# Storing the bf16 terms of q and k once and loading them twice, with the early stores of an attention and expert kernel in another order

## The chip, the cores and the metric

The kernel runs on one core of a Trainium2 chip. The core has a tensor engine (PE, with PEld for its weight loads), a vector engine (DVE), a scalar engine (ACT), GpSimd (POOL), a sync engine (SP) that does little but issue DMAs, and 16 DMA engines that all queues share. The metric is the device time of one execution in microseconds.

## What is computed

One transformer block with adaptive layer norm, on 1024 tokens of width 256. Cut to what matters:

```python
h = layernorm(x) * (1 + ca) + sa
q = (h @ Wq.T + bq) * 16 ** -0.5          # 16 heads of 16
k = h @ Wk.T + bk
v = h @ Wv.T + bv
scores = q @ k.T + slopes * -abs(i - j)   # 1024 x 1024 for each head
x = x + ga * (softmax(scores) @ v @ Wo.T + bo)
h = layernorm(x) * (1 + cb) + sb
x = x + gb * top4_of_16_experts(h)
```

## The kernel before

The first 44 us project x into q, k and v. The attention runs from there to about 255 us, head by head; the experts take the rest, and no line of theirs is touched.

**Terms.** q and k are split into three bf16 terms each (`qk_part[:, w, f, part, :]`, w 0 for q and 1 for k, f the half of the heads, 16 partitions a head). Products of terms stand in for a float32 product. The terms go from SBUF to DRAM (`q_rows`, `k_rows`: 96 rows of 1024 bf16 for each head, six blocks of 16) and come back with all rows of one head on neighbouring partitions. Which term stands in which block is told by `Q_PARTS` and `K_PARTS`: term 0 of q is stored three times, term 1 twice, term 2 once. `load_max(g)` (L502, L503) brings the first 64 rows twice, to partitions 0 to 63 and 64 to 127 of `qx` and `kx`, for the pass that finds the row maxima. `load_st(h)` (L509, L511) brings all 96 rows to `q_st` and to two copies in `k_st`, for the transposed scores. `load_al(h)` (L517) adds 24 rows of a bias from `al_rows`, which one store (L531) writes for all heads. `place_rows(g)` (L549) copies the row maxima, split by POOL in `split_rows` (L866), from `m_row` into two rows of `q_st`.

**Who stores what.** Heads 0 and 1: SP (`store_head`, L490, for the first four blocks, `store_terms` for the last two). Heads 2 to 7: ACT between its copies of v (four blocks), SP later (the last two). Heads 8 to 15: POOL, four DMAs in each of steps 0 to 2. Lines 455 to 456 are `store_term`.

**Order.** Every engine has its own program, run in order, with semaphore waits. The loop `steps` goes through c = -2 to 15. In step c PE computes the transposed scores of head c (L1460), the product with v (L1479), and the maxima scores of head c+2 (L1443, from the second pair of p on) and of head c+1 (the last two tiles, at p = 0). After the first two tiles of head c+2 it transposes the maxima of head c+1 (L1490); ACT copies them (L687), POOL splits them, SP places them. PE waits for `mx_in` (the four DMAs of `load_max`) before the first L1443 of a head and for `st_in`, `al_ld` and `m_in` before the first L1460. In step c SP issues, in this order: `load_st(c+1)`, `load_al(c+1)`, the store of head c-1's output (`os_rows`, L542), `place_rows(c+1)`, `load_max(c+3)`. DMAs of one engine go to one queue and are worked off in order on each DMA engine. From step 7 on POOL also loads the weights of one expert in each step (L901, L903; three in step 13), 672 KB each.

Of the kernel before, what the change touches and what calls it, by code (L numbers as in the profile page):

```python
# [10 lines left out]
BF16 = mybir.dt.bfloat16  # L11
# [6 lines left out]
P = 128  # L18
T = 1024
# [3 lines left out]
H = 16  # L23
# [14 lines left out]

Q_PARTS = (0, 1, 0, 1, 2, 0)
K_PARTS = (0, 0, 1, 1, 0, 2)  # L40
R_MX = 4 * D
# [71 lines left out]
def adaln_block(nc, a, out):  # L113
    with ExitStack() as ctx:
# [9 lines left out]

        q_rows = dram("q_rows", [H, 6 * D, T], BF16)
        k_rows = dram("k_rows", [H, 6 * D, T], BF16)
        al_rows = dram("al_rows", [6, H * NT, T], BF16)
# [324 lines left out]

        def store_term(eng, w, f, first, last, g):

            rows, part = ((q_rows, Q_PARTS[g]), (k_rows, K_PARTS[g]))[w]
            return eng.dma_start(rows[first:last, D * g:D * g + D, :],
                                 qk_part[D * first - P * f:D * last - P * f, w, f, part, :])

        @block.sync
        def _(sp):  # L460
# [23 lines left out]
            def store_head(h, w):  # L484

                rows, p0 = (q_rows, k_rows)[w], D * h
                for k in range(2):
                    src = (qk_part[p0:p0 + D, 0, 0, 0:2, :] if w == 0 else
                           qk_part[p0:p0 + D, 1, 0, k:k + 1, :].broadcast_to([D, 2, T]))
                    sp.dma_start(rows[h, 2 * D * k:2 * D * k + 2 * D, :].rearrange("(g r) t -> r g t", g=2),  # L490
                                 src).then_inc(qk_head[h], 16)

            def store_terms(n, first, last, terms):

                for w in range(2):
                    for g in terms:
                        store_term(sp, w, 0, first, last, g).then_inc(qk_stored[n], 16)
# [26 lines left out]
            for h in range(2):  # L524
                sp.wait_ge(qk_head[h], 16 * 4)
                load_max(h)
            sp.wait_ge(qk_split, 4)
            store_terms(0, 0, 2, (4, 5))
            sp.wait_ge(al_done, 1)
            sp.wait_ge(sign_done, 1)  # L530
            sp.dma_start(al_rows.rearrange("g r n -> r g n"), al_part[:]).then_inc(al_stored, 16)  # L531
            sp.wait_ge(qk_stored[0], 16 * 4)
            load_st(0)
            sp.wait_ge(al_stored, 16)
            load_al(0)
            load_st(1)
            load_al(1)

            def store_o(h):

                sp.wait_ge(o_evac, h + 1)
                sp.dma_start(os_rows[h].rearrange("r (g n) -> g r n", g=G), o_sb[:, h % 2, :]).then_inc(o_stored[h % 2], 16)  # L542

            def place_rows(g):

                sp.wait_ge(m_done, g + 1)
                for r in range(R_M):
                    to = R_QK + R_AL + r
                    sp.dma_start(q_st[to:to + 1, g % SLOTS, :].rearrange("p (i x) -> p i x", i=NT),  # L549
                                 m_row[:, r, :]).then_inc(m_in, 16)  # L550

            def step(c):
                if c == H - 2:
                    store_o(c - 1)
# [10 lines left out]
                if 0 <= c + 1 < H:  # L565
                    place_rows(c + 1)
                if 2 <= c + 3 < H:
                    if c == -1:
                        sp.wait_ge(qk_terms, 16 * 8)
                    if c + 3 == HT:  # L570
                        sp.wait_ge(qk_stored[2], 16 * 12)
                    sp.wait_ge(max_used, NT * c + 2 * NT)
                    load_max(c + 3)
                if c == -1:
                    sp.wait_ge(qk_split, 4)
                    store_terms(1, 2, HT, (4, 5))

# [24 lines left out]
        def _(act):  # L602
# [66 lines left out]
            for g in range(4):  # L669
                act.wait_ge(pe_group, V0 + g + 1)  # L670
                act.copy(v_all[:, 2 * g:2 * g + 2, :].rearrange("p t e -> p (t e)"), ps[:, bank_of[V0 + g], :]).then_inc(act_evac, 1)
                act.wait_ge(qk_second, 4)
                for w in range(2):
                    store_term(act, w, 0, 2, HT, g).then_inc(qk_terms, 16)
            make_bias_t(1)
# [103 lines left out]
        def _(pool):  # L779
# [75 lines left out]
            stage_v(1)  # L855
            for n in range(4, 8):
                rest_of(n, (n - 4) // 2, 1, n % 2)
                if n > 4:
                    third_part(n - 1, (n - 5) // 2, 1, (n - 1) % 2)

            def split_rows(g):
# [6 lines left out]

            split_rows(0)
            third_part(7, 1, 1, 1)  # L870
# [50 lines left out]
            def step(c):  # L921
# [8 lines left out]
                if 0 <= c < 3:  # L930
                    pool.wait_ge(qk_split, 8)
                    for w in range(2):
                        for g in (2 * c, 2 * c + 1):
                            store_term(pool, w, 1, HT, H, g).then_inc(qk_stored[2], 16)
                if c == 3:
# [7 lines left out]
                if c == C_EXP:  # L943

                    for h in range(2):
                        pool.wait_ge(qk_head[h], 16 * 4)
                    for n in range(3):
                        pool.wait_ge(qk_stored[n], 16 * (4, 4, 12)[n])
                    pool.wait_ge(qk_terms, 16 * 8)
                    pool.wait_ge(al_stored, 16)  # L950
                    pool.wait_ge(wo_done, 1)
                    pool.wait_ge(pe_group, N_GROUPS)
# [345 lines left out]
        def _(pe):  # L1298
# [147 lines left out]
            def scores_t(c, j, ch):  # L1446
# [3 lines left out]
                if u == 0:  # L1450
                    pe.wait_ge(st_in[s], 48 * (c // SLOTS) + 48)
# [205 lines left out]
```

## Time and profile before

| | us |
|---|---|
| median of 3 runs | 493.79 (493.55 to 493.92) |
| profiled execution, its own time | 489.35 |
| its span in the trace | 487.5 |
| PE busy | 401.6 (82% of the span) |
| DVE / ACT / POOL busy | 284.8 / 237.0 / 289.4 |
| DMA moved | 64.50 MB, mean 132 GB/s |

The profiled execution is 4.4 us shorter than the median; 1.85 us of its time lie outside the span. Differences worked out in the trace are therefore added to the median. PE is the busiest engine, but its share is a mean over the whole span. In the start, and at the first scores of a head, PE stands idle until a transfer lands; how often is read from PE's timeline, and what the transfer had to wait for from SP's timeline and the DMA share.

### The profile page before, as it was taken

The numbers are of one execution on the slowest core, as the hardware profiler recorded it, in microseconds if no ns is written. First come the engines' busy times: TensorE is split into PE (matmuls) and PEld (weight loads), VectorE is DVE, ScalarE is ACT, GpSimd is POOL, SyncE is SP. The second block draws the span as 40 slices with busy tenths as digits, with TensorE's granted clock in tenths as the row PEclk, the third lists the DMA queues.
The fourth block names the chain that finished last, engine by engine and source line by source line (L and its number), as shares of the span: only waits on it lengthen the run. The fifth ranks groups of instructions, "written<-read, shape, count | busy, mean of one in ns | idle before, by whom it ended". The sixth has DMA issues, their size and how long they took to land.

```text
span 487.5 us, 10785 instructions
## 1 busy us (share of the span) xinstructions
PE 401.6 (82%) x3712; PEld 218.0 (45%) x3714; DVE 284.8 (58%) x646; ACT 237.0 (49%) x503; POOL 289.4 (59%) x291
## 2 busy tenths in 40 slices
PE   4898749999999999999876627799899997999700
PEld 1764214344444444444435514366565554656400
DVE  3951948888998998999313784233333333333256
ACT  1273826777777777777870330233333333333211
POOL 5657617778889877777266001466566566665422
PEclk9598959999999999999995855899999999999955
DMA  7624735776333566658569900222222222232074
GB/s 217 257 39 153 239 117 137 176 190 203 109 106 105 155 170 168 170 159 239 165 151 298 279 5 2 73 77 73 64 84 66 75 67 66 75 76 56 0 273 157
DMA packets 38184, 64.50 MB, mean 132 GB/s; under 512 B 8177, under 2 KB 20903, under 8 KB 38014
## 3 DMA queue, kind: packets, MB, share of 16 engines
q1 hardware_dynamic: 25198, 34.95, 22.7%
q0 software_dynamic: 11584, 26.89, 21.6%
q10 hardware_dynamic: 1360, 2.10, 1.3%
q8 instruction: 27, 0.44, 0.4%
q14 instruction: 15, 0.12, 0.1%
HBM read 47.78 MB, written 18.01 MB: 135 GB/s over the span
## 4 chain that ended last, share of the span: by engine, by line
PE 50%; DVE 15%; DMA 13%; issue 8%; SPq 6%; ACT 5%; another core or an unknown queue 1%; POOL 0%; DVEq 0%; POOLq 0%; ACTq 0%
PE ps L1618 13%; PE ps L1460 7%; PE ps L1628 7%; PE ps L1479 7%; PE ps L1443 4%; ACT probs L703 3%; DVE x_sb L1290 3%; PE ps L1609 3%; DMA al_rows<-w_gu 3%; DVE junk L1096 3%; DMA x_sb<-in_x 2%; PE ps L1602 2%; DMA hT<-inv_rows 2%; PE ps L1465 2%; SPq L517 2%
## 5 line engine op out<-in xcount | busy, mean ns | idle before, releaser
L1096 DVE CUSTOM_DVE_ANT_0 junk<-ps,bias_t 128x1024 bf16<-128x1024 f32 x128 | 155.3, 1219 | 32.6 <-PE ps L1443 31.4
L703 ACT ACTIVATE probs<-ps 128x512 f32<-128x512 f32 x256 | 137.1, 603 | 47.5 <-DVE ps L1107 39.6
L1460 PE MATMUL ps<-q_st,k_st 122*32 122x512 bf16 x1024 | 84.5, 390 | 7.1 <-DMA q_st<-m_row 4.5
L1618 PE MATMUL ps<-w_gu,probs 128*128 x188 | 81.8, 558 | 0.0
L972 POOL DMA_INDIRECT probs<-xn_rows,bias_t x47 | 48.0, 1020 | 53.4 <-DVE bias_t L1259 38.6
L979 POOL DMA_INDIRECT z_rows<-probs,bias_t x47 | 48.1, 1023 | 49.9 <-DVE probs L1282 33.2
L1479 PE MATMUL ps<-probs,v_st 128*32 128x256 f32 x1024 | 66.7, 380 | 0.7 <-ACT probs L703 0.7
L797 POOL TENSOR_SCALAR bias_t<-dist,slopes 128x1920 f32<-128x1920 f32 x13 | 66.5, 5112 | 0.0
L1275 DVE TENSOR_TENSOR probs<-probs,ps 128x224 f32<-128x224 f32 x47 | 18.2, 387 | 81.5 <-ACT probs L765 56.6
L1443 PE MATMUL ps<-kx,qx 64*128 64x512 bf16 x256 | 44.2, 393 | 9.2 <-DMA kx<-k_rows 4.7
L754 ACT ACTIVATE probs<-ps,modc 128x128 f32<-128x128 f32 x47 | 21.5, 457 | 61.1 <-PE ps L1602 40.0
L1628 PE MATMUL ps<-w_dn,probs 112*128 x188 | 48.5, 380 | 0.5 <-ACT probs L760 0.5
L1460 PEld LDWEIGHTS ps<-q_st,k_st 122*32 122x32 bf16 x1024 | 23.6, 95 | 51.1 <-ACT probs L703 24.6
L1628 PEld LDWEIGHTS ps<-w_dn,probs 112*128 112x128 f32 x188 | 35.4, 189 | 20.5 <-issue 17.8
L765 ACT ACTIVATE probs<-ps 128x224 f32<-128x224 f32 x47 | 16.8, 358 | 53.8 <-PE ps L1618 46.3
L1618 PEld LDWEIGHTS ps<-w_gu,probs 128*128 128x128 f32 x188 | 32.1, 190 | 19.4 <-issue 18.4
L1479 PEld LDWEIGHTS ps<-probs,v_st 128*32 128x32 f32 x1024 | 30.6, 110 | 18.2 <-ACT probs L703 1.0
L1282 DVE TENSOR_TENSOR probs<-ps,gates 128x256 f32<-128x256 f32 x47 | 19.9, 424 | 16.2 <-remote 9.1
L1107 DVE TENSOR_TENSOR ps<-ps,bias_d 128x128 f32<-128x128 f32 x64 | 18.8, 294 | 16.6 <-PE ps L1460 16.6
L1443 PEld LDWEIGHTS ps<-kx,qx 64*128 64x128 bf16 x256 | 11.8, 93 | 36.7 <-issue 18.5
L1609 PE MATMUL ps<-ident,probs 128*112 128x128 f32 x94 | 19.1, 285 | 9.6 <-DVE probs L1275 6.0
L1465 PE MATMUL ps<-bias_d,ident 128*32 128x128 f32 x512 | 25.7, 277 | 0.0
(202 smaller groups left out, 486.1 us busy)
## 6 DMA issues: line engine op xcount, KB each, us to landing
k_st<-k_rows SPq DMA_DIRECT2D x32, 192.0 KB, 5.0
qx<-q_rows SPq DMA_DIRECT2D x32, 128.0 KB, 2.6
w_gu<-in_gate_proj POOLq DMA_DIRECT2D x16, 224.0 KB, 4.2
w_gu<-in_up_proj POOLq DMA_DIRECT2D x16, 224.0 KB, 5.1
w_dn<-in_down_proj POOLq DMA_DIRECT2D x16, 224.0 KB, 6.4
q_st<-q_rows SPq DMA_DIRECT2D x16, 192.0 KB, 3.7
kx<-k_rows SPq DMA_DIRECT2D x32, 64.0 KB, 2.7
os_rows<-o_sb SPq DMA_DIRECT2D x14, 128.0 KB
```

The lines of the kernel that those rows point to most:

```text
L703: act.activation(probs[:, j % 4, CH * ch:CH * ch + CH], ps_st[(NU * c + u) % 3], ACT.Exp).then_inc(exp_done, 1)
L797: pool.tensor_scalar(bias_t[:, h % 2, :], dist[:], slopes[:, h:h + 1], None, ALU.mult).then_inc(bias_p_done, 1)
L972: pool.indirect_dma_start(xg[:, n % 4, :], None, xn_rows, bass.IndirectOffsetOnAxis(ap=tab_i[:, n, 0:1].bitcast(U32), axis=0), bounds_chec ...
L979: pool.indirect_dma_start(z_rows, bass.IndirectOffsetOnAxis(ap=tab_i[:, n, 1:2].bitcast(U32), axis=0), y_sb[:, n % 4, :], None, bounds_che ...
L1096: dve.tensor_tensor_reduce(junk[:, n % 2, :], ps_max[n % 2].rearrange("p b n -> p (b n)"), bias_t[:, g % 2, off:off + T], 1.0, -3.0e38, AL ...
L1443: last = pe.matmul(ps_max[n % 2][:, r, :], qx[k, s, q * P:q * P + P], kx[k, s, :], start=True, stop=True)
L1460: last = pe.matmul(ps_st[n % 3][32 * g:32 * g + 32, :], k_st[0:R_ALL, ch, s, r:r + 32], q_st[0:R_ALL, s, CH * ch:CH * ch + CH], start=True ...
L1465: last = pe.matmul(ps_st[n % 3][32 * g:32 * g + 32, t * P:t * P + P], ident[:, 32 * g:32 * g + 32], bias_d[:, c % D_SLOTS, :], start=False ...
L1479: last = pe.matmul(ps_o[32 * g:32 * g + 32], v_st[:, c % 2, j, :], probs[:, j % 4, QG * g:QG * g + QG], start=(j == 0), stop=(j == NT - 1))
L1609: last = pe.transpose(ps[0:IH, 4 + (c - 1) % 2, kk * P:kk * P + P], hid[:, (c - 1) % 2, kk * IH:kk * IH + IH], ident[:])
L1618: last = pe.matmul(ps[:, 2 + c % 2, 0:2 * INTER], xT[:, c % 2, kk, :], w_gu[:, bass.ds(e, 1), kk, :].rearrange("p x n -> p (x n)"), start= ...
L1628: last = pe.matmul(ps[:, 6 + c % 2, 0:E], hidT[0:IH, c % 2, kk, :], w_dn[0:IH, bass.ds(e2, 1), kk, :].rearrange("p x n -> p (x n)"), start ...
```

## The change

- `q_rows` keeps four blocks a head, `k_rows` three: every term once, but term 0 of q twice. Terms 0 and 1 of q stand interleaved (row 2d + g), so that one DMA with runs of 4 KB stores both.
- The loads make the copies. For q: `q_rows[g, 0:2 * D, :]`, 32 rows, with a leading dimension of size 2 and stride 0 in front, onto 64 partitions. For k: 32 rows, each followed by a dimension of size 2 and stride 0. `load_max` stays at four DMAs of the same bytes; `load_st` becomes five DMAs from three.
- Heads 0 and 1: one store each for q and k instead of two. Heads 2 to 7: ACT issues three stores instead of eight, SP three instead of four. Heads 8 to 15: POOL issues two in each of steps 0 to 2 instead of four.
- `al_rows` is stored in two parts: 16 partitions (heads 0 and 1) right after `load_max(0)`, the other 112 after `load_al(1)`, just ahead of `load_max(2)`.
- `place_rows(0)` moves ahead of `load_st(1)`; POOL's `split_rows(0)` moves two tiles of splitting up.

```diff
-            return eng.dma_start(rows[first:last, D * g:D * g + D, :],
-                                 qk_part[D * first - P * f:D * last - P * f, w, f, part, :])
+        def store_q_pair(eng, f, first, last):
+            return eng.dma_start(q_rows[first:last, 0:2 * D, :].rearrange("h (d g) t -> h d (g t)", g=2),
+                                 qk_part[D * first - P * f:D * last - P * f, 0, f, 0:2, :].rearrange("p g t -> p (g t)"))
...
             def load_max(g):
                 for r in range(2):
-                    sp.dma_start(qx[R_MX * r:R_MX * r + R_MX, g % 2, :], q_rows[g, 0:R_MX, :]).then_inc(mx_in[g % 2], 16)
+                    sp.dma_start(qx[R_MX * r:R_MX * r + R_MX, g % 2, :],
+                                 q_rows[g, 0:2 * D, :].unsqueeze(0).broadcast_to([2, 2 * D, T])).then_inc(mx_in[g % 2], 16)
                     sp.dma_start(kx[R_MX * r:R_MX * r + R_MX, g % 2, :],
-                                 k_rows[g, 0:R_MX, CH * r:CH * r + CH]).then_inc(mx_in[g % 2], 16)
+                                 k_rows[g, D:3 * D, CH * r:CH * r + CH].unsqueeze(1)
+                                 .broadcast_to([2 * D, 2, CH])).then_inc(mx_in[g % 2], 16)
             def load_st(h):
-                sp.dma_start(q_st[0:R_QK, s, :], q_rows[h]).then_inc(st_in[s], 16)
+                sp.dma_start(q_st[0:R_MX, s, :],
+                             q_rows[h, 0:2 * D, :].unsqueeze(0).broadcast_to([2, 2 * D, T])).then_inc(st_in[s], 16)
+                sp.dma_start(q_st[R_MX:R_QK, s, :], q_rows[h, 2 * D:4 * D, :]).then_inc(st_in[s], 16)
                 for ch in range(NCH):
-                    sp.dma_start(k_st[0:R_QK, ch, s, :], k_rows[h]).then_inc(st_in[s], 16)
+                    sp.dma_start(k_st[0:R_MX, ch, s, :],
+                                 k_rows[h, D:3 * D, :].unsqueeze(1).broadcast_to([2 * D, 2, T])).then_inc(st_in[s], 16)
+                sp.dma_start(k_st[R_MX:R_QK, :, s, :],
+                             k_rows[h, 0:2 * D, :].unsqueeze(1).broadcast_to([2 * D, NCH, T])).then_inc(st_in[s], 16)
...
+            sp.wait_ge(qk_head[0], 16 * 2)
+            load_max(0)
+            sp.wait_ge(al_done, 1)
+            sp.wait_ge(sign_done, 1)
+            store_al(0, 0, 2)
+            sp.wait_ge(qk_head[1], 16 * 2)
+            load_max(1)
+            sp.wait_ge(qk_split, 4)
+            store_third(0, 0, 2)
+            sp.wait_ge(qk_stored[0], 16 * 3)
+            load_st(0)
+            sp.wait_ge(al_stored[0], 16)
+            load_al(0)
+            place_rows(0)
+            load_st(1)
+            load_al(1)
+            store_al(1, 2, H)
```

SP at the start, before, from the loads of head 1's maxima on (the numbers are the shape of the destination):

```order
L502 DMA qx<-q_rows 64x1024 [waits qk_head1]
L503 DMA kx<-k_rows 64x512
L502 DMA qx<-q_rows 64x1024
L503 DMA kx<-k_rows 64x512
L456 DMA q_rows<-w_gu 2x16x1024 [waits qk_split]
L456 DMA q_rows<-w_gu 2x16x1024
L456 DMA k_rows<-w_gu 2x16x1024 x2
L531 DMA al_rows<-w_gu 128x6x1024 [waits sign_done,al_done]
L509 DMA q_st<-q_rows 96x1024 [waits qk_stored0]
L511 DMA k_st<-k_rows 96x1024 x2
L517 DMA k_st<-al_rows 24x1x1024 [waits al_stored]
```

SP at the same place, after (`w_gu` holds `qk_part` and `al_part` at this time):

```order
L542 DMA al_rows<-w_gu 16x6x1024 [waits sign_done,al_done]
L510 DMA qx<-q_rows 64x1x1024 [waits qk_head1]
L512 DMA kx<-k_rows 64x1x512
L510 DMA qx<-q_rows 64x1x1024
L512 DMA kx<-k_rows 64x1x512
L461 DMA q_rows<-w_gu 2x16x1024 [waits qk_split]
L461 DMA q_rows<-w_gu 2x16x1024
L456 DMA k_rows<-w_gu 2x16x1024
L519 DMA q_st<-q_rows 64x1x1024 [waits qk_stored0]
L521 DMA q_st<-q_rows 32x1024
L523 DMA k_st<-k_rows 64x1x1024 x2
L525 DMA k_st<-k_rows 32x2x1024
```

The part of `al_rows` for heads 0 and 1 now stands ahead of head 1's loads, and one store of a term is gone. Next on SP, before, what stands between the bias rows of head 0 and the loads of head 2's maxima:

```order
L517 DMA k_st<-al_rows 24x1x1024
L509 DMA q_st<-q_rows 96x1024
L511 DMA k_st<-k_rows 96x1024 x2
L517 DMA k_st<-al_rows 24x1x1024 x2
L549 DMA q_st<-m_row 1x8x128 [waits m_done]
L549 DMA q_st<-m_row 1x8x128
L502 DMA qx<-q_rows 64x1024 [waits max_used,qk_terms]
```

And after:

```order
L532 DMA k_st<-al_rows 24x1x1024
L549 DMA q_st<-m_row 1x8x128 [waits m_done]
L549 DMA q_st<-m_row 1x8x128
L519 DMA q_st<-q_rows 64x1x1024
L521 DMA q_st<-q_rows 32x1024
L523 DMA k_st<-k_rows 64x1x1024 x2
L525 DMA k_st<-k_rows 32x2x1024
L532 DMA k_st<-al_rows 24x1x1024 x2
L542 DMA al_rows<-w_gu 112x6x1024
L510 DMA qx<-q_rows 64x1x1024 [waits max_used,qk_terms]
```

The placing of head 0's maxima moved ahead of head 1's loads, and the large part of `al_rows` came in front of head 2's first load.

## Rows read from the trace of the kernel before

**Rows 1.** The page, its slices of 12.2 us: PE busy and granted clock.
```profile
PE   4898749999999999999876627799899997999700
PEclk9598959999999999999995855899999999999955
```

**Rows 2.** PE's timeline, start and length in us; before the first L1490 (44 to 72).
```profile
44.56 0.91 PE L1443 MATMUL ps<-kx,qx 64*128 64x512 bf16 x4 [2.39 <-DMA kx<-k_rows]
...
63.77 0.61 PE L1443 MATMUL ps<-kx,qx 64*128 64x512 bf16 x2 [0.44 <-DVE mx L1096]
68.61 1.47 PE L1460 MATMUL ps<-q_st,k_st 122*32 122x512 bf16 x12 [4.24 <-DMA q_st<-m_row]
...
71.86 1.03 PE L1443 MATMUL ps<-kx,qx 64*128 64x512 bf16 x4 [0.91 <-DMA kx<-k_rows]
```

**Rows 3.** PE's timeline: the first maxima scores of heads 3, 4, 5, 8, 9 and 15.
```profile
84.66 0.61 PE L1443 MATMUL ps<-kx,qx 64*128 64x512 bf16 x4
...
97.06 0.61 PE L1443 MATMUL ps<-kx,qx 64*128 64x512 bf16 x4 [0.95 <-DMA kx<-k_rows]
...
108.94 0.60 PE L1443 MATMUL ps<-kx,qx 64*128 64x512 bf16 x4 [0.47 <-DMA kx<-k_rows]
...
143.19 0.60 PE L1443 MATMUL ps<-kx,qx 64*128 64x512 bf16 x4
...
154.59 0.61 PE L1443 MATMUL ps<-kx,qx 64*128 64x512 bf16 x4
...
222.93 0.60 PE L1443 MATMUL ps<-kx,qx 64*128 64x512 bf16 x4
```

**Rows 4.** The chain of waits, in order of time.
```profile
34.18 0.30 SPq L490
34.53 2.17 DMA k_rows<-w_gu
...
48.28 13.19 DMA al_rows<-w_gu
```

**Rows 5.** SP's own waits, 30 to 135 us: total, times, longest.
```profile
SPq L509 <- DMA k_rows<-w_gu: 8.5, 1, 8.5
```

**Rows 6.** SP's timeline of DMA issues, step 6: start, length.
```profile
140.44 0.32 SPq L509 DMA_DIRECT2D q_st<-q_rows  x1
...
141.75 1.58 SPq L517 DMA_DIRECT2D k_st<-al_rows  x2
143.59 0.58 SPq L542 DMA_DIRECT2D os_rows<-o_sb  x1
145.52 1.36 SPq L549 DMA_DIRECT2D q_st<-m_row  x2
146.92 0.51 SPq L502 DMA_DIRECT2D qx<-q_rows  x1
```

**Rows 7.** Windows: span, busy time of five engines, PE clock, share of 16 DMA engines, GB/s.
```profile
15.00:16.00 1.00, 1.00 (x8) 1.00 (x6) 1.00 (x4) 0.00 (x0) 0.00 (x0) 0.50 1.04 419
...
56.00:58.00 2.00, 1.20 (x6) 0.27 (x5) 1.81 (x5) 1.65 (x4) 2.00 (x2) 1.00 0.31 119
141.90:142.90 1.00, 1.00 (x26) 0.34 (x16) 1.00 (x4) 0.69 (x2) 0.00 (x0) 1.00 0.93 338
144.00:145.20 1.20, 1.14 (x25) 0.62 (x28) 1.20 (x4) 0.64 (x3) 0.41 (x2) 1.00 0.23 64
145.30:146.60 1.30, 1.30 (x24) 0.50 (x16) 1.01 (x2) 1.30 (x3) 1.30 (x2) 1.00 0.26 84
```

**Rows 8.** The page's DMA issues: size of one, median us from issue to landing.
```profile
qx<-q_rows SPq DMA_DIRECT2D x32, 128.0 KB, 2.6
w_gu<-in_gate_proj POOLq DMA_DIRECT2D x16, 224.0 KB, 4.2
```

**Rows 9.** POOL's timeline: the split of the first maxima, and the first expert load.
```profile
60.86 0.42 POOL L867 TENSOR_TENSOR m_row<-m_f,m_row 8x128 bf16<-8x128 f32 x1
...
162.56 0.81 POOL L901 DMA_DIRECT2D w_gu<-in_gate_proj  x1
```

More of the change, by code:

```diff
@@ L35 @@
 HT = P // D
[L39 to L40 removed]
+K_ROW = (D, 2 * D, 0)
+Q_ROW = {0: 2 * D, 2: 3 * D}
 R_MX = 4 * D
@@ L317, in adaln_block @@
         al_done = sem("al_done")
-        al_stored = sem("al_stored")
+        al_stored = [sem(f"al_stored{n}") for n in range(2)]
         v_done = sem("v_done")
@@ L451, in tiles, with store_k, store_q @@
                 tile(MAX_TILES // 4, k - MAX_TILES // 4 * 4)
-        def store_term(eng, w, f, first, last, g):
-            rows, part = ((q_rows, Q_PARTS[g]), (k_rows, K_PARTS[g]))[w]
-            return eng.dma_start(rows[first:last, D * g:D * g + D, :],
-                                 qk_part[D * first - P * f:D * last - P * f, w, f, part, :])
+        def store_k(eng, f, first, last, part):
+            b = K_ROW[part]
+            return eng.dma_start(k_rows[first:last, b:b + D, :], qk_part[D * first - P * f:D * last - P * f, 1, f, part, :])
+        def store_q(eng, f, first, last, part):
+            b = Q_ROW[part]
+            return eng.dma_start(q_rows[first:last, b:b + D, :], qk_part[D * first - P * f:D * last - P * f, 0, f, part, :])
+        def store_q_pair(eng, f, first, last):
+            return eng.dma_start(q_rows[first:last, 0:2 * D, :].rearrange("h (d g) t -> h d (g t)", g=2),
+                                 qk_part[D * first - P * f:D * last - P * f, 0, f, 0:2, :].rearrange("p g t -> p (g t)"))
         @block.sync
@@ L484, in store_head @@
             def store_head(h, w):
[L486 to L497, printed above, removed]
+                if w == 0:
+                    store_q_pair(sp, 0, h, h + 1).then_inc(qk_head[h], 16)
+                else:
+                    sp.dma_start(k_rows[h, D:3 * D, :].rearrange("(g r) t -> r g t", g=2),
+                                 qk_part[D * h:D * h + D, 1, 0, 0:2, :]).then_inc(qk_head[h], 16)
@@ L499, in load_max, with store_third @@
+            def store_third(n, first, last):
+                for part in (0, 2):
+                    store_q(sp, 0, first, last, part).then_inc(qk_stored[n], 16)
+                store_k(sp, 0, first, last, 2).then_inc(qk_stored[n], 16)
             def load_max(g):
                 for r in range(2):
-                    sp.dma_start(qx[R_MX * r:R_MX * r + R_MX, g % 2, :], q_rows[g, 0:R_MX, :]).then_inc(mx_in[g % 2], 16)
+                    sp.dma_start(qx[R_MX * r:R_MX * r + R_MX, g % 2, :],
+                                 q_rows[g, 0:2 * D, :].unsqueeze(0).broadcast_to([2, 2 * D, T])).then_inc(mx_in[g % 2], 16)
@@ L523, in _, with store_al @@
                     store_head(h, w)
[L524 to L542, printed above, removed]
+            def store_al(n, first, last):
+                r = slice(NT * first, NT * last)
+                sp.dma_start(al_rows[:, r, :].rearrange("g r n -> r g n"), al_part[r]).then_inc(al_stored[n], 16)
             def place_rows(g):
@@ L672, in _ @@
                 act.wait_ge(qk_second, 4)
-                for w in range(2):
-                    store_term(act, w, 0, 2, HT, g).then_inc(qk_terms, 16)
+                if g == 0:
+                    store_q_pair(act, 0, 2, HT).then_inc(qk_terms, 16)
+                elif g < 3:
+                    store_k(act, 0, 2, HT, g - 1).then_inc(qk_terms, 16)
             make_bias_t(1)
@@ L855, in _ @@
             stage_v(1)
[L856 to L859, printed above, removed]
             def split_rows(g):
@@ L867, in split_rows @@
                 pool.tensor_tensor(m_row[:, 1, :], m_f[:], m_row[:, 0, :], ALU.subtract).then_inc(m_done, 1)
-            split_rows(0)
+            for n in range(4, 8):
+                rest_of(n, (n - 4) // 2, 1, n % 2)
+                if n > 4:
+                    third_part(n - 1, (n - 5) // 2, 1, (n - 1) % 2)
+                if n == 6:
+                    split_rows(0)
             third_part(7, 1, 1, 1)
```

39 lines of the change are left out of this document (23 added, 16 removed).

## The prediction

> **What bounds the kernel now.** I read the page's slices first: PE is at nine tenths nearly everywhere, with a weak stretch at 49 to 73 us, where the clock is also at its lower level [rows 1]. PE's timeline then says what it waits for. Between 44 and 72 us it waits four times for DMAs or maxima; the largest is 4.24 us until head 0's maxima are placed, then 0.91 us for head 2's loads [rows 2]. After that the first maxima scores of a head (I call this moment X, with X0 = 71.86 for head 2) mark the pace: 84.66, 97.06, 108.94, and from there 11.4 us a head (154.59 - 143.19), up to X13 = 222.93 [rows 2, 3]. Waits of 0.95 and 0.47 us for DMAs stand at the second and third; the later ones have none [rows 3]. So DMAs decide the start, and PE with its partners the rest, as long as each head's loads land within its 11.4 us.
>
> The margin for that is read from SP's timeline. In the step with X = 143.19, `load_st` begins at X - 2.8, `place_rows` at X + 2.3, `load_max` at X + 3.7 [rows 3, 6]. Its four issues of some 0.6 us and a landing of 2.6 us [rows 8] end about X + 8.5, so 3 us are to spare.
>
> **How many DMA engines one transfer uses.** The windows show it [rows 7]. While `load_st` runs (96 rows outermost) the share of the 16 engines is 0.93. While `os_rows` is stored (destination 4x32x256) it is 0.26, which is four engines. While the bias rows run (source 6x4x1024) it is 0.23, near six engines with gaps. So a transfer is split along its outermost dimension, and a 4 there gives four engines. The new q loads read 2x32x1024: the copy dimension is outermost. I conclude two engines for each 128 KB. The new k loads have 32 rows outermost and keep 16.
>
> What the trace can't show is which two. The Trainium skill ("DMA: Bandwidth & Descriptors", section on why a DMA increments its semaphore by 16) has the count as the largest number up to 16 that divides the outermost size of both sides, and the engines as the lowest-numbered ones. The trace agrees on the count, with 0.26 for four.
>
> That small transfers share the same engines follows from a wait as well. SP waits 8.5 us for its term stores, until 57.1 us [rows 5]. By then two-engine stores of 4 x 64 KB (128 KB on each of the two), six-engine stores of 8 x 192 KB by ACT (256 KB) and 48 KB of loads were queued from about 38 us on. If all fall on the same engines, 432 KB (442 kB) in 19 us are 23.3 GB/s: one engine's pace. The other paces are 24.0 (119 GB/s at a share of 0.31), 21.1 (338 at 0.93, taken as 16 engines) and 26.2 (419 over 16) [rows 7]. The first is that of a few leftover engines late in the store of `al_rows`, which landed after 13.19 us although most of the rest was idle [rows 4, 7]. I take 25.0, the middle of 24.0 and 26.2, since no limit that all 16 share should bind two.
>
> **The change, part by part.** All of it is counted as KB on each of the two lowest engines.
>
> *Removed.* Stores: ACT 128 KB instead of 256, SP's third terms of heads 0 and 1 96 instead of 128, POOL 1792 KB instead of 3072 in three steps. Issues: ACT five fewer, POOL six fewer. Neither engine is waited for before the copy and split of head 0's maxima, which ends at 61.28 [rows 9] and follows PE's scores, so this is worth nothing.
>
> *Loads of one head, steady.* Before: `load_max` 2 x (8 + 4) = 24 KB, `load_st` 36, bias rows 16, `os_rows` 32, so 108 KB or 4.4 us of 11.4. After: `load_max` 2 x (64 + 4) = 136, `load_st` 64 + 4 + 8 + 8 + 8 = 92, bias rows 16, `os_rows` 32: 276 KB = 282.6 kB, at 25.0 GB/s 11.3 us. All of it is waited for within one head, in one queue, so the head can't be shorter than this and some 0.2 us of hand-over: 11.5 us. `load_st`'s two further issues (0.3 to 0.8 us each, by L509 and the bias rows [rows 6]) fall into 1.35 us in which SP waits for the maxima, at no cost; bounds 0 to 0.3 us, since `load_max` has its 3 us to spare.
>
> *X0.* The first loads are issued at 36.3 (34.18 for the single k store and its 2.1 us landing, [rows 4]), their data begin 1.5 us later. `load_max(0)` needs 139.3 kB = 5.6 us of engine time beside ACT's 131 kB = 5.2 us: landing between 43.5 (served first) and 49 (served last). Before, 24 KB beside the same queue landed 3 us later than alone (44.56, [rows 2]), so I take 47.5. Then `load_max(1)` 136, bias rows 12 and third terms 96 KB, 250 kB = 10.0 us, stored at 58 (before 57.1). `load_st(0)` and `load_al(0)` take 2.3 + 1.5 us of issue, until 62; the maxima, 3 us late with PE but two tiles of POOL's work earlier, are there at 61.5 (before 61.3, [rows 9]). Placing takes 1.4 us and lands near 66, while PE ends its own maxima scores near 67.5 (64.38 + 3). So the wait of 4.24 us goes, given back by the late start. Next on SP: `load_st(1)`, `load_al(1)`, the rest of `al_rows`, until 67.5, then `load_max(2)`. On the engines: 4.4 us for head 0 (to 64), 4.4 for head 1 (65 to 69), 84 KB of `al_rows` 3.4 (to 72.6), `load_max(2)` 5.6: 78.2, landed 79.0. X0 moves from 71.86 to 79.0: **+7.1 us**. At 26.2 GB/s +6.3, at 24.0 +7.5.
>
> *X0 to X3.* POOL's stores add 112 KB on each engine over three steps, 1.5 us a step: 13.0 us each, against 12.80, 12.40 and 11.88: **+1.9**. The six-engine third terms of heads 2 to 7 (48 KB, 2.0 us) fall into the first, where PE is just as late.
>
> *X3 to X7.* 4 x 11.5 against 45.65: **+0.4**.
>
> *X7 to X13.* POOL loads one expert a step, 672 KB over 16 engines = 43 kB = 1.7 us, first issued at 162.56 [rows 9]. Queues take turns on an engine, so a head needs 13.2 us against 11.39. The first load comes late in its step, so I count 5.5 of 6: **+10**. Cover for none of this is left, as PE, DVE and SP all wait for the same loads.
>
> Sum: 7.1 + 1.9 + 0.4 + 10 = 19.4. The profiled run would come from 489.35 to 508.8, the median from 493.79 to **513.2 us**. At 24.0 GB/s a head needs 12.0, 13.6 and 13.8 us, in sum +27 (521); at 23.3 +32 (526); at 26.2 11.0, 12.5 and 12.7, in sum +14 (508). These rates are the largest unknown. Nothing behind 255 us changes.
>
> **The rivals.**
>
> *A, the copies cost nothing (faster).* The stride-0 dimension isn't what the transfer is split by, and the loads use 16 engines as before. For it: same bytes, same row sizes. Against it: the 0.26 for an outermost 4 [rows 7]. Then maxima of head 0 are placed at about 60, `load_max(2)` is issued at 64.5 to 67, behind 1.34 MB of `al_rows` at 338 GB/s (4 us): landing 71, X0 -0.9; of the 2.9 us by which the next three heads exceed 11.4 each, a third returns. 493.8 - 2 = 491.8. The point from which it decides: `load_max` landing in under 3 us.
>
> *B, two engines, but quick ones.* Over 26 GB/s each, the loads of a head fit into 11.4 us with the expert's too; only the start is lost, +5 to +7, with up to 7 us from the experts' steps: 499 to 508. For it: 419 GB/s over 16 [rows 7] was shared. Against it: 24.0 in the same group. The Trainium skill (the same page, "Specifications") has about 27 GiB/s, 29 GB/s, for one engine. By it 282.6 kB take 9.7 us and an expert's 1.5, so nothing is lost after X3, and the time would be 499 as its estimate. No row here reaches it.
>
> *C, slower engines.* At 21.1 GB/s a head needs 13.6 us, 15.6 with the expert: 4 x 2.2 + 5.5 x 4.2 + 9 + 9.7 = +50, 544. Also into this case falls a clock that drops in PE's waits, as in the slices that follow the idle stretches of the start [rows 1, 2].
>
> **How the numbers follow.** The forecast (508 to 528) gets 0.62, B (498 to 508) 0.20, C (over 528) 0.08, A 0.10. A range of 500 to 528 leaves out A, C and a small part of B, 0.2 in all. A measurement of this kernel tells about 0.2% from no change. Slower: all but A and a remnant, 0.90. Faster 0.08, same 0.02.
>
> **What would show it.** In the new trace: landing of `qx<-q_rows` at 5 us and more instead of 2.6; a DMA share near 0.13 while it alone runs; PE waiting for `kx` or `qx` ahead of each head's first maxima scores, small for heads 6 to 9, near 2 us for heads 10 to 15; first scores of head 0 at 47 to 48, X0 near 79; no wait for `m_row` at the first L1460. X13 - X7 well over 68.3. If qx lands in under 3 us, A holds and the whole sum falls; if the heads run at 11.4 us to the end, B.

## The result, and the profile after

| | before | after |
|---|---|---|
| median | 493.67 us (4 runs) | 537.33 us (535.9 to 541.92, 4 runs) |
| profiled execution, its span | 489.35, 487.5 | 537.87, 536.1 |
| mean granted clock | 0.903 | 0.872 |
| first maxima scores of head 2 (X0) | 71.86 | 82.75 |
| X0 to X3, X3 to X7, X7 to X13 | 37.1, 45.7, 68.3 | 41.2, 49.5, 90.9 |
| last product with v (before L1479, after L1508) | 253.49 | 305.44 |

The ratio is 1.0897 (95%: 1.0841 to 1.0954): slower, as forecast, but by 43.7 us where 19.4 were forecast, and outside the range of 500 to 528. Some executions fall into a slower state of the chip, so the ratios here and below are of the fast ones alone, and only e6's trace is of a slow one (533.03 us). In the numbering of the changed kernel the maxima scores are L1472 (before L1443), the transposed scores L1489 (L1460), the loads of `qx` and `kx` L510 and L512.

The page's slices, PE busy and granted clock, to set beside [rows 1]: the weak stretch at the start is longer, and from the middle of the attention on (slices 15 to 22, 188 to 295 us) few nines are left.

```profile
PE   4994728979899877869594864679999989898900
PEclk8696957989999997979798995589999979999955
```

PE's waits between 30 and 310 us (total, times, longest). The first stands in the place of 4.7 us in four waits for `kx` in before. The second is at the last head, where before had none; the 4.24 us for `m_row` at the first L1460 [rows 2] are gone:

```profile
PE ps L1472 <- DMA kx<-k_rows: 44.7, 13, 10.8
PE ps L1489 <- DMA q_st<-m_row: 7.2, 1, 7.2
```

PE's timeline (start, length, wait in brackets): the first scores of head 0 (44.56 in [rows 2]), the first L1489, which no longer waits for `m_row`, then X0, X4, X7, X9, X13, and the last head's L1489.

```profile
49.30 1.04 PE L1472 MATMUL ps<-kx,qx 64*128 64x512 bf16 x4 [7.85 <-DMA kx<-k_rows]
69.63 1.47 PE L1489 MATMUL ps<-q_st,k_st 122*32 122x512 bf16 x12
82.75 1.04 PE L1472 MATMUL ps<-kx,qx 64*128 64x512 bf16 x4 [10.77 <-DMA kx<-k_rows]
136.89 0.60 PE L1472 MATMUL ps<-kx,qx 64*128 64x512 bf16 x4 [1.48 <-DMA kx<-k_rows]
173.48 0.60 PE L1472 MATMUL ps<-kx,qx 64*128 64x512 bf16 x4 [0.53 <-DMA kx<-k_rows]
203.74 1.04 PE L1472 MATMUL ps<-kx,qx 64*128 64x512 bf16 x4 [5.72 <-DMA kx<-k_rows]
264.37 1.04 PE L1472 MATMUL ps<-kx,qx 64*128 64x512 bf16 x4 [5.46 <-DMA kx<-k_rows]
292.85 1.47 PE L1489 MATMUL ps<-q_st,k_st 122*32 122x512 bf16 x12 [7.20 <-DMA q_st<-m_row]
```

A window (columns as in [rows 7]) in which a q load runs alone:

```profile
170.00:171.00 1.00, 1.00 (x16) 0.37 (x16) 0.90 (x3) 0.80 (x2) 1.00 (x1) 1.00 0.13 51
```

The share of 0.13 is two of 16 engines, and 51 GB/s over two are 25.5 GB/s each. The number of engines and their rate were therefore right (25.0 had been taken); what was built on them fell short.

Where the 48.6 us between the spans lie: X0 +10.9, X0 to X3 +4.1, X3 to X7 +3.9, X7 to X13 +22.6, from X13 to the last product with v +10.5 (41.07 against 30.56), behind that -3.3 (230.7 against 234.0). The -3.3 are two parts. From the last product with v to the first expert's matmul it takes 46.4 us where before takes 53.9: PE's 4.45 us wait for `attT` is gone, as PE comes later itself. From there to the end it takes 4.1 us more, for a reason that was not looked for. So most of what the last head loses by its wait of 7.2 us comes back.

### The profile page after: what moved, and what is told of

The parts are those of the page before. It is cut to its first block, busy times and chain, and to the rows that moved or that the text cites. A ratio compares the mean times of both kernels' runs of the same rounds, so it can differ in the third digit from the quotient of the medians.

```text
span 536.1 us, 10802 instructions
## 1 busy us (share of the span) xinstructions
PE 410.1 (76%) x3712; PEld 220.1 (41%) x3714; DVE 284.8 (53%) x646; ACT 239.3 (45%) x503; POOL 285.9 (53%) x285
## 3 DMA queue, kind: packets, MB, share of 16 engines
q10 hardware_dynamic: 850, 1.31, 0.8%
## 4 chain that ended last, share of the span: by engine, by line
PE 37%; DMA 24%; DVE 13%; SPq 11%; issue 5%; ACT 4%; POOL 3%; another core or an unknown queue 3%; ACTq 0%; POOLq 0%; DVEq 0%
DMA kx<-k_rows 16%; PE ps L1647 12%; PE ps L1657 6%; PE ps L1508 3%; PE ps L1638 3%; PE ps L1489 3%; SPq L510 3%; DVE x_sb L1319 3%; DVE junk L1125 3%; PE ps L1472 2%; DMA k_rows<-w_gu 2%; SPq L512 2%; SPq L549 2%; PE ps L1631 2%
## 5 line engine op out<-in xcount | busy, mean ns | idle before, releaser
L1489 PE MATMUL ps<-q_st,k_st 122*32 122x512 bf16 x1024 | 86.0, 405 | 9.5 <-DMA q_st<-m_row 7.2
L1647 PE MATMUL ps<-w_gu,probs 128*128 x188 | 83.2, 566 | 0.0
L1472 PE MATMUL ps<-kx,qx 64*128 64x512 bf16 x256 | 45.3, 406 | 49.5 <-DMA kx<-k_rows 44.7
L1508 PE MATMUL ps<-probs,v_st 128*32 128x256 f32 x1024 | 71.1, 400 | 0.7 <-ACT probs L729 0.7
L780 ACT ACTIVATE probs<-ps,modc 128x128 f32<-128x128 f32 x47 | 21.5, 457 | 58.7 <-PE ps L1631 47.8
L1489 PEld LDWEIGHTS ps<-q_st,k_st 122*32 122x32 bf16 x1024 | 23.4, 98 | 52.5 <-issue 22.7
L1472 PEld LDWEIGHTS ps<-kx,qx 64*128 64x128 bf16 x256 | 11.0, 94 | 78.3 <-DMA kx<-k_rows 40.6
L1508 PEld LDWEIGHTS ps<-probs,v_st 128*32 128x32 f32 x1024 | 32.1, 115 | 20.3 <-issue 2.8
L887 POOL CAST m_row<-m_f 8x128 bf16<-8x128 f32 x16 | 4.5, 280 | 53.4 <-ACT m_f L713 53.4
L1494 PE MATMUL ps<-bias_d,ident 128*32 128x128 f32 x512 | 27.0, 288 | 0.0
```

The lines of the kernel that those rows point to most:

```text
L780: act.activation(xT[:, (c + 1) % 2, 0, :], ps[:, 0, 0:P], ACT.Identity, bias=modc[:, 2, 0:1], scale=modc[:, 3, 0:1]).then_inc(xT_act, 1)
L1472: last = pe.matmul(ps_max[n % 2][:, r, :], qx[k, s, q * P:q * P + P], kx[k, s, :], start=True, stop=True)
L1489: last = pe.matmul(ps_st[n % 3][32 * g:32 * g + 32, :], k_st[0:R_ALL, ch, s, r:r + 32], q_st[0:R_ALL, s, CH * ch:CH * ch + CH], start=True ...
L1494: last = pe.matmul(ps_st[n % 3][32 * g:32 * g + 32, t * P:t * P + P], ident[:, 32 * g:32 * g + 32], bias_d[:, c % D_SLOTS, :], start=False ...
L1508: last = pe.matmul(ps_o[32 * g:32 * g + 32], v_st[:, c % 2, j, :], probs[:, j % 4, QG * g:QG * g + QG], start=(j == 0), stop=(j == NT - 1))
L1647: last = pe.matmul(ps[:, 2 + c % 2, 0:2 * INTER], xT[:, c % 2, kk, :], w_gu[:, bass.ds(e, 1), kk, :].rearrange("p x n -> p (x n)"), start= ...
```

## The experiments

The kernels ran on several chips, on which the kernel before takes 477 to 497 us in the median; each is compared with runs of before on its own chip. The numbers used across chips are differences in the attention, X's above all: the pace of 11.39 us a head is the same on all of them. "Ready" is when PE was free for the first maxima scores (42.17 in before: 44.56 less its wait of 2.39). The ratio of e11 is that of 508.8 to 492.8 us and has no interval. The stages vary from trace to trace: X3 to X7 is 45.7 and 47.1 us in two traces of before, and 49.5 and 51.1 in after and e4, whose programs are the same up to there.

| | ratio to before (95%) | X0 - ready | X0 to X3 | X3 to X7 | X7 to X13 |
|---|---|---|---|---|---|
| before | | 29.7 | 37.1 | 45.7 | 68.3 |
| after | 1.0897 (1.0841 to 1.0954) | 41.3 | 41.2 | 49.5 | 90.9 |
| e1_q_two_loads | 1.0131 (1.0070 to 1.0192) | 34.1 | 40.8 | 45.6 | 68.3 |
| e2_before_max2 | 1.0788 (1.0709 to 1.0866) | 43.7 | 45.0 | 51.4 | 81.1 |
| e3_before_both2 | 1.0982 (1.0894 to 1.1069) | 44.0 | 44.5 | 53.2 | 88.2 |
| e4_after_experts_late | 1.0535 (1.0458 to 1.0613) | 41.5 | 41.9 | 51.1 | 73.3 |
| e5_before_max2_early_load | 1.0732 (1.0647 to 1.0817) | 43.2 | 47.8 | 57.1 | 76.6 |
| e6_after_early_load | 1.0987 (1.0886 to 1.1088) | 41.9 | 45.1 | 56.9 | 90.4 |
| e7_two_loads_al_behind | 1.0070 (1.0017 to 1.0123) | 31.2 | 40.9 | 45.6 | 68.3 |
| e8_two_loads_max_first | 1.0122 (1.0084 to 1.0161) | 27.0 | 44.4 | 45.6 | 70.2 |
| e11_before_max2_three | 1.03 | 43.0 | 41.6 | 45.5 | 70.3 |
| e12_after_three | 1.0603 (1.0426 to 1.0781) | 41.4 | 38.2 | 48.3 | 84.4 |
| e13_before_join | 1.0000 (0.9928 to 1.0072) | 29.4 | 36.6 | 45.5 | 68.3 |
| e15_two_loads_order_join | 1.0118 (1.0018 to 1.0217) | 27.0 | 45.2 | 45.6 | 70.5 |
| e16_before_order_alone | 1.0140 (1.0076 to 1.0204) | 32.6 | 41.3 | 46.8 | 68.3 |
| e17_two_loads_old_order | 1.0051 (1.0010 to 1.0092) | 28.3 | 40.5 | 45.6 | 68.3 |

### Are the two engines the cause?

```diff
-                    sp.dma_start(qx[R_MX * r:R_MX * r + R_MX, g % 2, :],
-                                 q_rows[g, 0:2 * D, :].unsqueeze(0).broadcast_to([2, 2 * D, T])).then_inc(mx_in[g % 2], 16)
+                    for i in range(2):
+                        b = R_MX * r + 2 * D * i
+                        sp.dma_start(qx[b:b + 2 * D, g % 2, :], q_rows[g, 0:2 * D, :]).then_inc(mx_in[g % 2], 16)
```

and the same in `load_st`, with the wait counts.

> The changed kernel, but each q load with the copy dimension is replaced by two DMAs of 32 rows each, 64 KB, which read the same rows; bytes, stores and order stay as changed, and SP issues two DMAs more in load_max and one more in load_st. Theory (the two engines that the copy dimension leaves to a transfer are the cause): with 32 rows outermost each part spreads over 16 engines, load_max lands in 2 to 3 us again, heads run at 11.4 us (X7 to X13 68 to 70 us against 90.9), the first maxima scores of head 2 stand at 71 to 73, and the time is 489 to 495. Rival (the added issues of load_st on SP, the early store of a part of al_rows, or the k loads with their copy dimension inside are the cause): these all stay or grow, and the time stays over 515.

It is the cause of most of it: every head from X3 on takes 11.4 us again. Issue to landing of the q loads, by this kernel's page (the page of after gives no median for them):

```profile
qx<-q_rows SPq DMA_DIRECT2D x64, 64.0 KB, 2.1
```

But X0 still came at 80.4, not 71 to 73, with a wait of 7.2 us (4.1 of the 8.5 us against before are a later ready, 46.27), and the kernel stays 1.3% slower. This rest is taken up below. The reverse edits, the copy dimension put into the loads of the kernel before:

> The kernel before with one edit: the two q loads of load_max read 32 rows with a leading copy dimension of 2 instead of 64 rows; the blocks of the kernel before hold these same terms in the same order, so the result is the same, and so are bytes and number of DMAs. Theory (load on the two engines, as a sum for each head): load_max 136 KB, load_st 36, bias rows 16, output 32, 220 KB or 225 kB on each of the two, at the 25.5 GB/s that two engines showed 8.8 us, which fits into a head of 11.4. So X3 to X7 stays at 45 to 47 us, X7 to X13 is 69 to 76, head 2's first maxima scores come 4 to 8 us later, and the time is 498 to 508. Rival (not the sum but each transfer of its own is what holds PE up, as load_max lands late whenever it takes 5 us and more): waits for qx and kx at every head, X3 to X7 over 49, time over 515.

> The kernel before with both q loads, of load_max and of load_st, read with the leading copy dimension; load_st gains one DMA for its last 32 rows. Stores, k loads and the order of stores stay as before. Theory (the two engines): 220 KB and 62 more in load_st, 280 KB a head on each of the two, as in the changed kernel: heads of 12 us and more, X3 to X7 48 to 51, X7 to X13 87 to 93, time 528 to 540. Rival (the new order of stores or the k loads carry a good part of the loss): under 515.

The second (e3) held in the main: +9.8%, X7 to X13 88.2, X3 to X7 53.2 where 48 to 51 were expected. The loads alone make a loss of the size of the whole. For the first (e2) the rival came true: waits at nearly every head, 51.4 us from X3 to X7, +7.9%. With 220 KB a head on the two engines, 8.8 us of work, a head takes 12.3 to 12.6 us between X4 and X7. The sum, on which the prediction rested, does not explain that. SP's issues in one step of this kernel, and windows of the same step:

```profile
171.91 1.37 SPq L550 DMA_DIRECT2D q_st<-m_row  x2
173.32 0.56 SPq L502 DMA_DIRECT2D qx<-q_rows  x1
175.04 0.48 SPq L504 DMA_DIRECT2D kx<-k_rows  x1
```

```profile
173.00:174.00 1.00, 1.00 (x12) 0.32 (x12) 0.68 (x3) 1.00 (x4) 1.00 (x1) 1.00 0.02 4
174.00:175.00 1.00, 1.00 (x24) 0.56 (x24) 1.00 (x4) 0.68 (x3) 1.00 (x1) 1.00 0.01 4
178.00:179.00 1.00, 1.00 (x20) 0.31 (x8) 0.89 (x3) 1.00 (x3) 1.00 (x1) 1.00 0.13 49
```

```profile
169.93 0.61 PE L1444 MATMUL ps<-kx,qx 64*128 64x512 bf16 x4 [1.14 <-DMA kx<-k_rows]
182.53 0.60 PE L1444 MATMUL ps<-kx,qx 64*128 64x512 bf16 x4 [1.18 <-DMA kx<-k_rows]
```

For 2 us the DMA engines are all but idle; the k loads take the next two, and then only two engines work. They wait for an order of events: at X = 169.93 the previous head's maxima scores are done, POOL splits the maxima, SP places them at X + 2.0 and issues `load_max` at X + 3.4. Its data come from about X + 5 on and need 5.5 us on two engines by themselves (139 kB at 25.5 GB/s); from X + 9 on `load_st` shares the engines. The last has landed at X + 12.6, which is the next X. The buffer is free only after the head before, so each head's load starts from the head's own beginning. This reads as a closed chain of 12.3 to 12.6 us a head. Whether it is the chain or the two engines' load that counts, the next runs test.

### Chain or sum?

First try: `load_max(c+3)` issued ahead of `place_rows(c+1)`.

> The kernel before with the two-engine q loads in load_max alone, as in e2_before_max2, and in each step from 0 on the order of load_max(c+3) and place_rows(c+1) on SP exchanged, so that the load is issued about 3 us earlier after the first maxima scores of a head (X). The result is the same. New theory (a chain, not the sum: X, then split and place of the maxima, then load_max issued at X + 3.4, its data from X + 5.6 on, 6.3 us on two engines, landing at X + 12.4, which is the next X): without the 3 us of placing in it the chain is 9.5 us, shorter than the 11.4 that PE needs, so X3 to X7 falls from 51.4 to 45.6 to 47, X7 to X13 from 81.1 to 69 to 75, and the time from 517.7 to 500 to 508. Rival (the two engines themselves can't deliver a head's loads faster than every 12.3 us, whatever the order): X3 to X7 stays at 49 to 51 and the time over 513.

> The changed kernel with the same exchange: in each step from 0 on SP issues load_max(c+3) before place_rows(c+1). Chain alone as the cause: as in e5_before_max2_early_load, all heads near 11.4 to 11.8 us up to X7, X7 to X13 75 to 80, time 515 to 522. Sum on two engines (276 KB a head, 11.1 us at 25.5 GB/s and 3 us more beside an expert load) as the cause: X3 to X7 stays at 47.5 to 50, X7 to X13 at 84 to 91, and the placed maxima, now behind the load on the same two engines, are waited for instead: time 530 to 540. I expect the sum to hold here, since 11.1 us leave nothing over.

For the changed kernel the second case held, but for X3 to X7, which took 56.9 us where 47.5 to 50 were expected. For e5 the gain did not come, and the rival had only the time right (over 513): X3 to X7 is longer than without the exchange (57.1 against 51.4; one head of 19.2 us in it, the others 12.4 to 12.9), and the pace stays at 12.6 to 12.9 up to X13. PE's wait had only changed its place:

```profile
178.30 0.83 PE L1463 MATMUL ps<-q_st,k_st 122*32 122x512 bf16 x12 [1.13 <-DMA q_st<-m_row]
```

The placed maxima now stand behind the load on the same two engines, and the next head's scores need them. Either order has both transfers in the chain. The experiment didn't take the chain apart; a third buffer does, which lets the load start a head earlier:

```diff
-        qx = sb("qx", [P, 2, T], BF16)
-        kx = sb("kx", [P, 2, CH], BF16)
+        qx = sb("qx", [P, 3, T], BF16)
+        kx = sb("kx", [P, 3, CH], BF16)
...
+                if 3 <= c + 3 < H:
+                    sp.wait_ge(max_used, NT * c + NT)
+                    load_max(c + 3)
```

(at the head of the step, in place of the one at its end that waits for `NT * c + 2 * NT`).

> As e2_before_max2 (the kernel before, load_max with two-engine q loads), but with three buffers for qx and kx instead of two, so that load_max(c+3) no longer waits for the maxima of head c+1 and is issued a whole head before it is needed; bytes, sizes and engines of all transfers stay. e5_before_max2_early_load had left the chain closed, since placed maxima and loads share the two engines and both stood in it. Theory (a chain of release, place, issue and a transfer of 6 us sets 12.3 us a head, not the sum of 220 KB on the two engines, 8.8 us): the waits for kx go from X3 on, X3 to X7 is 45.6 to 46.5 instead of 51.4, X7 to X13 68.3 to 71 instead of 81.1, time 497 to 504. Rival (the two engines are short of capacity at 220 KB a head): X3 to X7 stays at 49 to 51, time over 510.

> The changed kernel with three buffers for qx and kx in the same way; 276 KB a head stay on the two engines. Sum theory: 11.1 us at 25.5 GB/s fit just below the 11.4 that PE needs, so X3 to X7 falls to 46 to 48 from 49.5; beside an expert load (3.1 us more) the sum is 14 us, so X7 to X13 is still 80 to 88 instead of 90.9; time 525 to 534. Chain alone as the cause of the changed kernel's loss after X3: X3 to X7 45.6 to 46 and X7 to X13 68 to 73, time 508 to 516.

With the same 220 KB on the same two engines all waits for `kx` are gone from X1 on and the pace is 11.4 us from X3 to X10: chain, not sum. (The last three heads before X13 take 12.0 to 12.1 us, with waits of 0.7 to 0.8 us for `m_row`. The expected times had a chip in mind on which before takes 480 us; the difference here, 16.0 us, compares with 17 to 24.) In the changed kernel 276 KB are another matter: X3 to X7 goes from 49.5 only to 48.3, no more than traces differ, and X7 to X13 from 90.9 to 84.4. The paces are near those that the sum gave (46 to 48 and 80 to 88), and the waits stand at `m_row` now (0.2 to 3.7 us). The time fell between: 523.05 us, just below the sum's 525 to 534. So in the changed kernel from X3 to X7 no run separates the chain from the load on the two engines; by rate that load is 11.1 us a head, and 12.1 were measured with the third buffer.

### The expert loads

> The changed kernel with all expert loads issued after the loop of steps instead of one in each step from 7 on; what they load is the same, but the first experts wait for it at the end, so the total time says little and the pace of the heads is what counts. Theory (expert loads take their share of the two engines, some 3.1 us a head): X7 to X13 is 6 x 12.0 to 12.4 = 72 to 75 us instead of 90.9, and the wait of 7.2 us for the last head's placed maxima goes. Rival (the later heads are slow for a reason of their own, the clock or the longer queue of output stores): X7 to X13 stays at 85 or more.

X7 to X13 fell by 17.6 us, to 73.3: 2.9 us a head, where the prediction had 1.7. Windows of the changed kernel suggest why, a head's loads and an expert's together (198 to 199), and PE waiting for what was queued behind (202 to 203):

```profile
198.00:199.00 1.00, 0.01 (x4) 0.00 (x0) 0.06 (x2) 1.00 (x4) 0.65 (x2) 1.00 1.04 218
202.00:203.00 1.00, 0.00 (x0) 0.00 (x0) 0.00 (x0) 0.00 (x0) 0.00 (x0) 0.50 0.21 78
```

All 16 engines are busy and move 218 GB/s, 13.6 GB/s each, where alone they reach 25.5. At 13.6 GB/s the 43 kB of an expert's weights on one engine would take 3.2 us, an estimate near the 2.9. That this makes the 2.9 us is a reading of the windows; no run takes it apart. PE's granted clock also falls to 0.50, its 1.2 GHz level, in the longer of these waits, and the first scores after it take 1.04 us for 0.61. The wait of 7 us for the last head's `m_row` did not go (6.95 us here), which had been expected, so the expert loads don't cause it. In the changed kernel SP issues `place_rows(15)` at 284.43, behind POOL's two loads of `attT` (896 KB, 283.55 and 284.13); in before it stood ahead of them (238.32 against 240.17).

### The rest: 1.3% with repaired loads

> As e1_q_two_loads (the changed kernel with each q load as two DMAs of 32 rows), but the large store of al_rows is issued after load_max(2) instead of ahead of it. Theory (what is left of the loss in e1_q_two_loads is head 2's load queued behind 1.34 MB of that store): the wait of 7.2 us before head 2's first maxima scores falls to 3 us or less, and the time by 3 to 5 us against e1_q_two_loads, to about that of the kernel before (+0.1 to 0.7%). Rival (the rest comes from the added issues and the stores of the terms on two engines): less than 1.5 us of change.

> As e1_q_two_loads, but head 2's load_max stands right behind place_rows(0), ahead of load_st(1), load_al(1) and the large store of al_rows. If head 2's load is what PE waits for in the start: it is issued at 67 instead of 72 and finds empty engines, lands at 70 to 71, PE's wait of 7.2 us goes, and the time is 7 to 10 us below e1_q_two_loads, that is 0.2 to 0.9% below the kernel before. Rival (a later wait takes its place, for load_st(1), which is now behind, or for the maxima): 0 to 3 us below e1_q_two_loads.

Moving the large store of `al_rows` behind head 2's load took 2.9 us off X0 - ready and nearly half of the ratio's excess away (1.3% to 0.7%, with intervals that overlap). Moving head 2's load to the front instead gave X0 without a wait (27.0) and gave nearly all of that back one head later, in a wait of 7.8 us for head 1's placed maxima behind that store. Then both halves of the change apart, with a trace of the kernel before from the same chip:

> The kernel before with the change's order alone: al_rows stored in two parts (heads 0 and 1 behind load_max(0), the rest ahead of load_max(2)), place_rows(0) ahead of load_st(1), POOL's split_rows(0) two tiles up; terms stored and loaded as before. The two kernels with repaired q loads and the change's stores reached head 5's first maxima scores 72.1 and 74.9 us after PE was free for the first ones, against 66.8 before. If the order is the cause of that: here 71 to 75 us as well, and 0.7 to 1.5% slower than before. If the stores or the k loads are: 65 to 68 us, and within 0.4% of before.

> The counterpart: terms stored once and q loads as two DMAs of 32 rows (e1_q_two_loads), but the order of before (al_rows in one store behind the terms, place_rows(0) behind load_al(1), split_rows(0) at its old place). If the order was the cause of the rest: head 5's first maxima scores 66 to 68 us after PE was free, time within 0.5% of before. If the stores and more loads are: 71 to 75 us and 0.7 to 1.5% slower.

> The kernel before, unchanged, for a trace from the same chip as the two runs beside it. All kernels that ran on the chips where before takes 480 us needed about 138 us from the first expert's matmul to the last, those on the others 152 to 157. If that is the chip: here either value, with the two beside it at the same; the head's pace, 11.39 us, is the same on all.

The order alone costs 1.4% (0.8 to 2.0), 6.7 us; the terms stored once and loaded with 16 engines, in the order of before, 0.5%, with lower bound 0.1%. So the two halves have their own prices. Both together had 1.3% (e1, 0.7 to 1.9 on another chip), so the prices need not add up. Head 5's first maxima scores stand 73.9 us after ready with the new order alone, 68.8 with the terms alone, 65.6 in before on this chip. A part of the order's price, 3.2 of the 8.4 us, is there at X0, and is seen in windows of 68 to 70 us, e16 first, the kernel before (e18) second:

```profile
68.00:70.00 2.00, 0.00 (x0) 0.00 (x0) 0.00 (x0) 0.00 (x0) 0.00 (x0) 0.50 1.00 314
```

```profile
68.00:70.00 2.00, 1.89 (x24) 0.87 (x24) 1.15 (x2) 0.82 (x2) 0.00 (x0) 0.50 0.60 165
```

Between SP's issue of the store (66.29) and of head 2's load (66.85) nothing waits, and the load's data come behind 1.34 MB; PE waits 7.54 us:

```profile
74.30 1.03 PE L1453 MATMUL ps<-kx,qx 64*128 64x512 bf16 x4 [7.54 <-DMA kx<-k_rows]
```

What the new order wins, maxima of head 0 placed 3.4 us earlier (61.89 against 65.30), is less than that. The other 5.2 us come between X0 and X3, nearly all of them as one wait of 5.01 us for head 5's own `kx` (115.62), when the large store has long landed and POOL's last stores of terms (issued from 106.2 on) are under way. Why it falls there was not looked into. The last two tried to turn the findings into a gain:

> The kernel before, with POOL's two loads of attT (896 KB) issued behind the store of inv_rows instead of ahead of the reciprocals. In the trace of before the chain at the end of the attention runs os_rows, sum_c, inv_rows (5.0 us to landing, behind those 896 KB), hT (8.6 us), attT, and PE waits 4.45 us for it. If the queue in front of inv_rows is what costs: it lands in 2 to 3 us, hT 2 us earlier, PE's wait falls to 1.5 to 3 us, time 0.3 to 0.6% below before. Rival (attT now lands as late as hT did, the bytes before the last one are the same): within 0.2%.

> The changed kernel with each q load as two DMAs (e1_q_two_loads) and three changes of order: load_max(2) right behind place_rows(0) as in e8_two_loads_max_first; the large store of al_rows behind place_rows(1), since it and load_st(1) ahead of it had cost 7.8 us for the placed maxima of head 1; POOL's loads of attT behind the store of inv_rows as in e13_before_join, since place_rows(15), issued 2.6 us later than before, had fallen behind them and cost 5.4 to 6.4 us. Expected: X0 no later than in e8_two_loads_max_first (27 us after PE is free for it), X1 12.8 to 14 us later, no wait of more than 2 us for m_row at the last head; 0.8 to 2% below the kernel before. Rival (a saving in the start is returned at the next stage, as in e8_two_loads_max_first): between 0 and 0.7% above it.

Neither beats the kernel before. In e13 `attT` still made PE wait 4.27 us (4.45 before), as the rival had it: the bytes ahead of the last one are the same. In e15 the last head's wait fell to 1.31 us, but head 3's load, behind the store now, waited 7.5 us: the fourth order of the start in which the 1.34 MB are paid by whoever stands behind them. The last head's shorter wait (5.1 us less than in e8) brings only a part of its length: from X13 to the first expert's matmul e15 takes 81.3 us, e8 84.7 and the kernel before 82.3 and 84.4 in two traces. PE waits for `attT` when it comes earlier (2.65 us in e15, nothing in e8).

## Why the prediction was right and wrong

- *Two engines for a leading copy dimension*: right, 0.13 of the DMA time and 51 GB/s. The count by the rule of the Trainium skill that it drew on ("DMA: Bandwidth & Descriptors", section on why a DMA increments its semaphore by 16) holds here for a dimension of stride 0 too; which two engines, no run shows. Rival A is out as to the loads; had it held, its 491.8 would still have been too low, since e1_q_two_loads, which is that case, is 1.3% slower than before.
- *25.0 GB/s an engine*: right for a load alone (25.5). The 29 GB/s of the Trainium skill ("DMA: Bandwidth & Descriptors", "Specifications") are not reached, and rival B falls with them.
- *Start of head 0 at 47 to 48; no wait for the first L1460; X0 +7.1*: 49.30, 1.3 us past it; right, no wait; and +10.9. The store of `al_rows` was counted as 3.4 us of two engines' time; the order that puts it there costs 6.7 us in all even with 16-engine loads (e16). Also SP's issues took up to 3.3 us each in the start (L512 at 44.25), where 0.6 had been assumed.
- *X0 to X3 +1.9*: +4.1, with a wait of 3.30 us at X2; this was not taken apart.
- *X3 to X7 +0.4*: +3.9. The failed step is "3 us to spare", which was read from [rows 6] for a landing of 2.6 us and then not redone for one of 8 us. Place, issue, start and transfer add up to 12.3 to 12.6 us a head in e2, and a third buffer took that away (e11). The sum of 11.5 looked at the engines' work and not at when it could begin. The chain was in the rows already: X + 3.7 for the first issue, 1.5 us from issue to data and 5.6 us for the transfer are 10.8 of 11.4 us, before any landing. How much of the +3.9 it is in the changed kernel stays open, as e12 with a third buffer is only 1.2 us shorter there; what the rest is beyond 11.1 us of load a head was not found.
- *X7 to X13 +10*: +22.6. The second failed step is the term of 1.7 us for an expert's load: it cost 2.9 us a head (17.6 us in all, e4), with 13.6 GB/s an engine in the windows where the loads meet. The other 5.0 us stay without the expert loads: 12.2 us a head, as from X3 to X7.
- *`load_st`'s further issues at no cost*: right in the steady state (e1: 11.4 us), wrong for the last head. There SP needs 6.3 us from the output's store (L573) to `place_rows(15)`, before 3.6, and so stands behind POOL's loads of `attT`; with these moved the wait falls to 1.31 us (e15).
- *Nothing behind 255 us changes*: +10.5 from X13 to the last product with v, of which 3.3 returned.
- *Sum*: X3 to the end had been given 10.4 us and took 33.7. Of the 23.3 us between, the pace of a head makes 7.8 (12.2 to 12.4 us for 11.5), the expert loads 8.2 (17.6 for 9.4), and what stands behind X13 7.2. Rival C had the size nearly (544) from a slower engine, a cause that a load alone doesn't show.
- *Two readings of the rows*: between 44 and 72 us PE waits nine times and not four (three times for DMAs, six for DVE's maxima), and the clock is at its lower level only from 61 us on, not from 49 [rows 1]. No term hung on either.

What stays open: which part of the terms' half costs its 0.5%; e17 shows longer first waits (first scores of head 0 at 47.93 against 43.20) and a wait of 5.97 us for the last head's `m_row`, but load count, k loads and stores were not taken apart. Of the last head's wait most comes back here too: e17 is 9.4 us behind e18 at the last product with v, counted from ready, and 3.8 at the first expert's matmul.

## What to carry to other kernels

When a transfer becomes slower, redo the chain that releases it (free buffer, issue, first data, transfer, use) before summing the load on its engines: a closed chain longer than the stage's pace costs in every round, and an idle engine in the middle of it is its sign. A copy dimension in a DMA belongs inside a larger one (with 32 rows outside it `kx` landed in 2.3 us, e1's page), or the transfer is made two. And a large store has to be paid by whoever stands behind it in the queue, so look for a place where nobody does, not for one where another waits.

## What the hardware showed unexpectedly

The chips differ in one part of this program. The unchanged kernel took 151.5 us from the first expert's matmul (307.37) to its last group (458.90) on the first chip and 137.9 us (304.94 to 442.88) on another, with the last product with v at 253.49 and 253.16; the experiments fall on one side (137.9 to 139.3) or the other (151.1 to 157.0) with their chip. What differs between the chips was not looked for. Two versions are therefore to be compared on one chip only. The two ends on that other chip, in PE's timeline:

```profile
304.94 1.32 PE L1618 MATMUL ps<-w_gu,probs 128*128 x3
442.88 1.50 PE L1628 MATMUL ps<-w_dn,probs 112*128 x5 [0.42 <-ACT probs L760]
```
